# A decoder kernel of two layers: the order of three pieces of the mixing stage on VectorE and TensorE

## The reference, cut to what matters

```python
xa = _ln(x, ln1_g, ln1_b);  xx = _shift(xa)          # shift: the position before
xk, xv, xr = xa * time_mix_k + xx * (1 - time_mix_k), ...
k, v, r = xk @ att_Wk.T, xv @ att_Wv.T, xr @ att_Wr.T
rwkv = sigmoid(r) * _wkv(time_decay, time_first, k, v)   # weighted mean over the past
x = x + rwkv @ att_Wo.T
xc = _ln(x, ln2_g, ln2_b);  xx2 = _shift(xc)
xk2, xr2 = xc * cm_k + xx2 * (1 - cm_k), xc * cm_r + xx2 * (1 - cm_r)
kk = square(relu(xk2 @ ffn_Wk.T))                    # hidden width 1024
return x + sigmoid(xr2 @ ffn_Wr.T) * (kk @ ffn_Wv.T)
```

## Time and profile before

| what | value |
|---|---|
| three runs, us | 2000.43, 1997.98, 1991.75; median 1997.98 |
| profiled execution: time, us | 1993.02 |
| its span, us | 1991.2 |
| mean granted TensorE clock | 0.942 |
| busy share of the span: PE, DVE, ACT, POOL | 85%, 63%, 55%, 28% |
| the mixing stage | about 1058 to 1490 us |

### The profile page before, as it was taken

How to read it: one execution, slowest core, us unless ns; L and a number is a source line. 1 busy time by engine, 2 the same in 40 slices (tenths; PEclk the granted TensorE clock), 3 DMA queues, 4 the chain that set the end, 5 groups by cost and what they waited for, 6 DMA issues and landing times. The chain is left out here.

```text
span 1991.2 us, 40593 instructions
## 1 busy us (share of the span) xinstructions
PE 1691.7 (85%) x13412; PEld 1393.7 (70%) x13412; DVE 1248.1 (63%) x4276; ACT 1103.6 (55%) x2520; POOL 566.1 (28%) x719
## 2 busy tenths in 40 slices
PE   6577777774899999999956999999988999999963
PEld 5455555553688888889944877787766888888842
DVE  6689999858211111111118999999936988888856
ACT  2299999920222222223325666666636888888845
POOL 3433233230211111101025566666520000000017
PEclk9899999976899999999977999999998999999975
DMA  3100010025455555558930000000001000000002
GB/s 117 47 26 25 19 26 18 2 80 183 135 180 187 181 186 183 185 174 267 323 129 14 19 22 22 22 22 22 12 12 40 23 23 23 23 23 23 2 1 85
DMA packets 102046, 154.64 MB, mean 78 GB/s; under 512 B 5760, under 2 KB 85504, under 8 KB 101088
## 3 DMA queue, kind: packets, MB, share of 16 engines
q1 hardware_dynamic: 85600, 125.25, 19.1%
q0 software_dynamic: 6480, 17.70, 3.0%
q10 hardware_dynamic: 9776, 9.31, 1.3%
HBM read 134.54 MB, written 17.69 MB: 76 GB/s over the span
## 5 line engine op out<-in xcount | busy, mean ns | idle before, releaser
L1836 ACT ACTIVATE moe_hT<-moe_p_h,lane_a 128x256 f32<-128x256 f32 (+1 forms) x344 | 131.4, 433 | 370.3 <-PE moe_p_h L1788 370.0
L1788 PE MATMUL moe_p_h<-moe_gT,moe_w 128*128 128x256 f32 (+1 forms) x1376 | 256.1, 345 | 0.8 <-issue 0.8
L1330 ACT ACTIVATE xb_pr<-xb_sc,xb_nmax 128x256 f32<-128x256 f32 x512 | 225.5, 502 | 50.7 <-DVE xb_nmax L1407 50.6
L1798 PE MATMUL moe_p_y<-moe_w,moe_hT 128*128 128x256 f32 x1136 | 252.3, 379 | 0.0
L1788 PEld LDWEIGHTS moe_p_h<-moe_gT,moe_w 128*128 128x128 f32 x1376 | 227.6, 192 | 25.7 <-issue 1.2
L1798 PEld LDWEIGHTS moe_p_y<-moe_w,moe_hT 128*128 128x128 f32 x1136 | 212.5, 190 | 27.1
L1407 DVE CUSTOM_DVE_ANT_0 xb_sc<-xb_p_s,xb_neg 128x256 f32<-128x256 f32 x512 | 187.0, 420 | 47.2 <-PE xb_p_s L1182 43.7
L837 ACT ACTIVATE xa_pr<-xa_sc,xa_nmax 128x256 f32<-128x256 f32 (+1 forms) x512 | 204.0, 453 | 17.6 <-DVE xa_nmax L917 17.2
L1705 POOL DMA_INDIRECT moe_gx<-moe_tokens,moe_source_i x71 | 67.4, 949 | 457.2 <-PE moe_p_t L1775 400.6
L1956 DVE COPY moe_gT<-moe_p_t 128x512 f32<-128x512 f32 (+1 forms) x43 | 25.7, 599 | 232.3 <-PE moe_p_t L1775 232.3
L1981 DVE TENSOR_TENSOR moe_gy<-moe_p_y,lane_a 128x256 f32<-128x256 f32 x71 | 27.5, 421 | 229.1 <-PE moe_p_y L1798 229.1
(11 more groups left out here) (331 smaller groups left out, 3454.3 us busy)
## 6 DMA issues: line engine op xcount, KB each, us to landing
moe_w<-in_L_ffn_w_dram SPq DMA_DIRECT2D x86, 1024.0 KB
moe_rows_out<-moe_gy ACTq DMA_DIRECT2D x28, 256.0 KB
X<-in_x_dram SPq DMA_DIRECT2D x4, 1024.0 KB, 10.9
xa_ctx<-in_ctx_turned_dram SPq DMA_DIRECT2D x16, 256.0 KB, 2.8
moe_tokens<-moe_XN_s SPq DMA_DIRECT2D x16, 256.0 KB, 2.1
xb_ctx<-in_ctx_turned_dram SPq DMA_DIRECT2D x16, 256.0 KB
xb_raw<-in_fside_BxSxS_dram SPq DMA_DIRECT2D x16, 256.0 KB
out_dram<-X SPq DMA_DIRECT2D x2, 1280.0 KB, 5.2
```

The lines of the kernel that those rows point to most:

```text
L1330: last = act.activation(pr[:, n % RB, e, :], sc[:, n % RB, e, :], ACT.Exp, bias=nmax[:, n % RB, e:e + 1], scale=-1.0)
L1788: last = pe.matmul(p_h[n % 3][:, k * width:(k + 1) * width], w1[:, r, ic, (2 * n + k) * P:(2 * n + k + 1) * P], gT[:, r % 2, ic, 0:width], ...
L1798: last = pe.matmul(p_y[:, t * D:(t + 1) * D], hT[:, hc, t * P:(t + 1) * P], w2[:, r, hc, :], start=(hc == 0), stop=(hc == HC - 1))
L1836: last = act.activation(hT[:, 2 * n + k, 0:width], p_h[n % 3][:, k * width:(k + 1) * width], ACT.Gelu, bias=b1[:, bass.ds(e * HC + 2 * n + ...
```

## The change

Three pieces of the stage trade places. On PE the turning of the next input (`turn_x`) goes behind the receptance projection. On DVE the function `run_sums` is cut into `sum_weights` and `sum_values`, and the difference and mixes of the channel mix come between the two; and `mix_time` takes a list of parts, so that the key mix stands ahead of `finish_time` and the value and receptance mixes behind it. The wait for `dif_ready` goes with part 0. The prologue ahead of the loop is changed in the same way for the time mixes. No operation is added or left out.

```diff
--- before.py
+++ after.py
@@ -2262,8 +2262,6 @@
                     turn(zn, p_t, s_["turned_m"])
                 if not first(b):
                     values_out(b - 1, 1)
-                if has_next(b, 2):
-                    turn_x(b + 2, b + 1)
                 if ended(b):
                     break
                 pe.wait_ge(s_["mixed2_ready"], 2 * b + 1)
@@ -2272,6 +2270,8 @@
                         last = pe.matmul(p_y[:, t * D:(t + 1) * D], mixed2[:, 1, ic, t * P:(t + 1) * P], w[:, 4, ic, :],
                                          start=(ic == 0), stop=(ic == DC - 1))
                 last.then_inc(s_["r2_ready"], 1)
+                if has_next(b, 2):
+                    turn_x(b + 2, b + 1)
                 pe.wait_ge(s_["mixed2_ready"], 2 * b + 2)
                 if first(b):
                     pe.wait_ge(s_["loaded_fk"], 16)
@@ -2440,12 +2440,13 @@
                 dve.tensor_scalar(scale_x[:, 1, :], aggr[:, 0, :, 1], 1.0 + LN_EPS, LN_EPS * LN_EPS, ALU.mult, ALU.add)
                 dve.tensor_scalar(mean_x[:, :], aggr[:, 0, :, 0], -1.0, None, ALU.mult).then_inc(s_["measured_x"], 1)
 
-            def mix_time(n):
-                dve.wait_ge(s_["dif_ready"], n + 1)
-                for m, nm in enumerate(("time_mix_k", "time_mix_v", "time_mix_r")):
+            def mix_time(n, parts):
+                for m in parts:
+                    if m == 0:
+                        dve.wait_ge(s_["dif_ready"], n + 1)
                     if since(n, 1):
                         dve.wait_ge(s_["projected"], 3 * n - 2 + m)
-                    mix(mixed[:, m, :, :], nm, xa, dif, s_["mixed_ready"])
+                    mix(mixed[:, m, :, :], ("time_mix_k", "time_mix_v", "time_mix_r")[m], xa, dif, s_["mixed_ready"])
 
             kk = p_k[:, :].rearrange("p (c n) -> p c n", c=DC)
 
@@ -2461,7 +2462,7 @@
                     wait_alone(dve, s_["stood_v"], (s_["keep_lead"], n), (s_["read_lead"], n))
                 dve.tensor_tensor(lead[:, :, :], kk, run[:, :, 0:S], ALU.subtract).then_inc(s_["lead_ready"], 1)
 
-            def run_sums(n):
+            def sum_weights(n):
 
                 dve.wait_ge(s_["keep_ready"], n + 1)
                 if since(n, 1):
@@ -2469,6 +2470,9 @@
                 for c in range(DC):
                     last = dve.tensor_tensor_scan(den[:, c, 1:S + 1], fall[:, c, :], gain[:, c, :], 0.0, ALU.mult, ALU.add)
                 chain.done(last)
+
+            def sum_values(n):
+
                 dve.wait_ge(s_["gain_v_ready"], n + 1)
                 if since(n, 1):
                     dve.sem_inc(s_["stood_v"], 1)
@@ -2509,14 +2513,16 @@
 
             combine(0, 0, 0)
             measure_x(0)
-            mix_time(0)
+            mix_time(0, (0, 1, 2))
             run_max(0)
             combine(1, 1, 0)
             measure_x(1)
-            run_sums(0)
+            sum_weights(0)
+            sum_values(0)
             invert(0)
+            mix_time(1, (0,))
             finish_time(0)
-            mix_time(1)
+            mix_time(1, (1, 2))
             chain.close()
             for b, h, s in turns(dve, drain=True, ahead=2):
                 if has_next(b):
@@ -2535,7 +2541,7 @@
                     combine(b + 2, s, h + 1)
                     measure_x(b + 2)
                 if has_next(b):
-                    run_sums(b + 1)
+                    sum_weights(b + 1)
                 if not ended(b):
                     dve.wait_ge(s_["xc_ready"], b + 1)
                     chain.done(dve.tensor_tensor(dif2[:, :, :], xc[:, :, 1:S + 1], xc[:, :, 0:S], ALU.subtract))
@@ -2544,14 +2550,18 @@
                         wait_alone(dve, s_["stood_v"], (s_["r2_ready"], b), (s_["hidden"], HC // 2 * b))
                     for m, nm in ((1, "cm_r"), (0, "cm_k")):
                         mix(mixed2[:, m, :, :], nm, xc, dif2, s_["mixed2_ready"])
+                if has_next(b):
+                    sum_values(b + 1)
                 if not first(b):
                     close_batch(b - 1)
                 if has_next(b):
                     invert(b + 1)
                 if has_next(b, 2):
-                    mix_time(b + 2)
+                    mix_time(b + 2, (0,))
                 if has_next(b):
                     finish_time(b + 1)
+                if has_next(b, 2):
+                    mix_time(b + 2, (1, 2))
                 chain.close()
             dve.wait_ge(s_["added"], B)
 
```

## The result

| | before | after |
|---|---|---|
| median of 6 runs each, us | 1995.86 | 2006.72 |
| lowest to highest, us | 1991.75 to 2000.43 | 2002.62 to 2015.18 |
| profiled execution, us (its span) | 1993.0 (1991.2) | 2015.18 (2013.4) |

The ratio of after to before is 1.0068, with a 95% interval of 1.0049 to 1.0087: the change makes the kernel 0.7% slower, 10.9 us between the medians. The time lies inside the forecast's range (1987 to 2009), at the end that rival C had opened, and not where the forecast put it (1998, as before). Among the six runs of after, the profiled one is the slowest, so its trace shows the loss larger than usual: 22 us instead of 11.

What follows compares the result with a forecast made beforehand. DVE was taken as the pace, with PE having some 2.3 us of slack a turn. The steps summed to -0.2 to 0 us a turn, -2.6 to 0 over 13 turns, so the median forecast was 1998 us, range 1987 to 2009.

Steps and rivals of the forecast that it cites:

- rival C: Channel mixes: POOL's "a" starts before the second (receptance) mix, delaying projection, turning and dif; 2003 to 2009 us, chance 0.25.
- the two PE waits: PE waits 0.92 us for mixed_out before the output projection, 1.40 us for yn before turning the input, each turn.
- Without a hole: DVE's instructions in a turn follow without gaps; its one wait for another unit is 0.54 us before the combine.
- Step 1: Gate ahead of two time mixes: DVE 0; output projection starts at 7.0 to 7.2, its 0.92 us wait gone.
- rival B: POOL's "a" or dif slips past its DVE meeting, saving 0.72 to 1.02 us a turn; 1985 to 1994, chance 0.20.
- Step 2: Channel mixes ahead of value scans: mixes start 1.16 us sooner, third still meets POOL's "a"; DVE 0.
- Step 3: Input turned behind receptance projection: PE's 1.40 us wait becomes about 0.9 on the mix; DVE -0.2 to 0 a turn.
- Rival A: Mixing stage: PE was the pace, so both its waits, 28.2 us at most, come back; 1970 us, chance 0.04.
- Rival D: Ahead of the channel mixes: dif2 waits for xc in many turns, 13 x 0.5 us; 2005, chance 0.03.

Runs made afterwards that it cites:

- e10: Changed kernel with POOL's "a" (denominator) waiting until DVE has done the receptance half of the channel mixes; 1995.2 us, 1.0013 of before.
- e4: Changed kernel with POOL's gathers for batch b + 3 issued ahead of its two additions to X; 1961.4 us, 0.9847 of before.
- e7: Kernel before with only gated and mixed_out moved ahead of two time mixes; 1980.3 us, 0.9942 of before.
- e2: Changed kernel with the PE edit undone (input turned ahead of the receptance projection again), both DVE edits kept; 1982.9 us, 0.9954 of before.
- e8: Kernel before with only the channel mixes moved ahead of the value scans; 1998.5 us, 1.0018 of before.
- e11: Changed kernel with 20 filling transposes on PE ahead of the receptance projection, in turns 1 to 3 only; 1997.6 us, 1.0033 of before.
- e1: Kernel before with only the next input's turning moved behind the receptance projection on PE; 2017.3 us, 1.0132 of before.

## Why the prediction was right or wrong

- **What bounds the kernel** (DVE is the pace, the two PE waits are slack): right for before. The end of both waits gave nothing by itself in e10. "Without a hole" leaves out DVE's short waits for its own results (0.18 us ahead of the channel mixes, for one), which belong to its pace. And it holds only with late gathers: in e4 PE is the pace.
- **Step 1**, gate ahead: PE's side was right (the output projection starts at 7.05 us in a settled turn of after; walked 7.0 to 7.2). "DVE: 0" fails for the edit alone: e7 is 0.6% faster. It makes PE and ScalarE earlier, and in every second turn meetings and the combine's wait fall away (read for e2 above). That is near to the mechanism of rival B, in e2 and e7, but not in after.
- **Step 2**, channel mixes ahead of the scans: right. e8 differs by 0.2%, and a meeting with a scan costs what one with a mix does.
- **Step 3**, turning behind the receptance projection: this is the step that failed. The walk found the margin (0.22 us between the second mix and "a"; 0.21 in a settled turn), and its sum took the margin to hold in every turn. In ten turns of each of after's two profiled executions it did not. The sum had -0.2 to 0 us for a turn; measured are 14.9 us more in 13 turns (357.7 against 342.8), +1.15 for a turn. The wait that step 3 made 0.9 us is 2.0 to 2.7 us in the caught turns, and the projection behind it, walked with 1.8 us, takes 2.4 to 3.8 us in all of them but one. The walk of one turn could not show what varies between turns: the idle time of DVE at 1263.05, which the trace of before has, is longer than the margin.
- **Rival C** named the mechanism, the place and the point from which it decides. Its price, 0.4 to 0.84 us a turn, is near the mark for one catch with the clock up (0.6 us in e11, some 0.3 us of DVE's idle time in it). Two things were off. It left out the clock: a caught turn in after costs 0.7 to 2.5 us, since the wait is followed by slower matmuls (up to 3.78 instead of 1.89 us), and dif slips into the next turn, past gated, mixed_out and the gathers. And its chance, 0.25, took the margin as a coin to be tossed once for the kernel. It is put to the test in each turn, and one caught turn brings on the next.
- **Sum and range**: 1998 was forecast, and 2006.7 measured, inside C's 2003 to 2009. That is partly luck: C's price a turn was too low, and not every turn is caught. With the catch alone taken away (e10), the measured time is 0.1% from before, so the rest of the sum stands.
- **Rival A** (1970 us at most if both PE waits came back) was rightly kept low for this change, but e4 shows that the time was there to be had, once the gathers no longer tie DVE down. **Rival D** did not show: in the turns shown of after the mixes wait for dif2 alone (0.18 us), and dif2 not for xc.

## What to carry to other kernels

Where a change hangs a producer on a consumer with a margin of some tenths of a microsecond, walk what happens if it is missed all the way round the loop, through the DMAs, until it comes back to the same margin: if it arrives late there too, one miss is a lasting state and its price is that of all turns. Look through all turns of the trace for an idle time as long as the margin, not through one. Price a new wait of TensorE with the rate of the matmuls behind it, and not with its length alone. And issue gathers ahead of work that nobody waits for: alone it gave 0.75% here, and it turned the three edits from a loss of 0.7% into a gain of 0.8%.

## What was not expected of the hardware

- In a stage in which TensorE is busy for 91% (311.69 of 342 us), a single wait of 2.0 to 2.7 us was in most turns followed by matmuls at a lower granted clock, 0.50 to 0.79 over the projection, which then took 2.4 to 3.8 us instead of 1.89. After waits as long the clock stayed at 1.00 seven times: 2.73 us at 1363.35 in after, 2.05 at 1260.46 and 2.73 at 1397.06 in e11, and 2.44 in four turns of e1 (at 1193.73, 1308.53, 1336.53 and 1417.64). Waits of 0.7 to 1.2 us in e10 were never followed by a lower clock.
- In e7 it came in two turns in which PE waited 1.40 us for yn and then under 0.4 us; the windows view of one of them, between 1181.0 and 1184.4 us, shows a clock of 0.61. So the length of the last wait alone doesn't decide.
- A scan with two SBUF inputs is held up by POOL as a mix is: 2.29 us for two instead of 1.25.
- DVE idles for 0.26 us at one fixed instruction of its program, and for 0.35 us more than usual at another, in all kernels that have the same instructions there, and the profile names no other engine and no DMA that it waits for. The cause is open.
- The same program can have two lasting ways of running, 26.2 and 28 us a turn, and changes from one to the other in the middle of an execution. Into the slow one it fell, from settled turns, where DVE idles as said; out of it it came, but for one case, behind a wait after which the clock was 1.00.
